# A decoder layer on one core: the last key tile turned as the fourth, a wait of GpSimd for VectorE's low half, masks on VectorE, and a written-out first trip

## The chip, the cores and the metric

One core of a Trainium2 chip. The metric is the device time of one execution in microseconds, as the median of several. The kernel is written with one hand-made instruction order for each engine: TensorE (PE), VectorE (DVE), ScalarE (ACT), GpSimd (POOL) and SyncE (SP), which issues all DMAs. Engines meet by semaphores alone.

## What is computed

A decoder layer of three blocks, each with residual and layer norm, on x of 4 x 256 x 512: a gated MLP that keeps half of the gate's entries by size, cross-attention to 4 x 1601 context rows, and a top-1 expert. The change touches the cross-attention and what stands on either side:

```
q = rmsnorm(x @ Wq.T) per head (32 heads of 128), k = rmsnorm(ctx @ Wk.T), v = ctx @ Wv.T (8 heads)
scores = q @ k.T / sqrt(128) + mask          # 256 x 1601 for each of 4 x 32 heads
out = softmax(scores) @ v, then @ Wo.T
x = layernorm(x + out)
```

## The kernel before

The program runs stage by stage: `gate_and_up`, `keys_and_values` (with the top-k counts on VectorE), `down_and_norm`, `queries`, `attention`, `output_and_experts`. A stage's loads and first steps are called inside the stage ahead of it, by functions named `early_...`.

`attention` (line 1943) works on 32 items (batch and key head), each of two units; a unit is 2 of the 4 query heads of the item, 512 query columns in four tiles j = 0 to 3 of 128. In fp16 pairs of high and low part a product is three matmuls (`product`, lines 206 to 208). For one tile j:

- TensorE scores 128 queries against all keys into four banks (`score`); these banks exist once, so the next score waits for VectorE.
- VectorE subtracts the mask and takes the minimum (`subtract_mask`, L2473), ScalarE takes the exp with its sum (`exp`, L2405).
- The probabilities have to be turned, keys onto partitions. There are NT = 13 key tiles of 128, the last with 65 keys. The first 7 go through DMA transposes in fp16: the high half is made by GpSimd for even j (L2284) or ScalarE for odd j (L2290), the low half by VectorE for even j (`halves_lo_dve`, L2294) or GpSimd for odd j (L2299), and SyncE issues a transposing DMA for each (`turn_halves`, L2184). The other 6 are turned by TensorE (`transpose_p`, L2571) into one of 3 banks, cast by ScalarE (`split_p`, L2434) and their low parts taken by VectorE (L2507).
- For the tile of the last 65 keys GpSimd repeats the keys behind the end (`repeat_tail`, L2277) and ScalarE copies the high part of 32 rows and of one row into pT_lo (L2438), so that two matmuls do for three (L2595, L2597).

The order of the loop stands in a few tables. A unit has 13 positions. At each, every engine does what the tables name. `P_AT` says at which positions the product takes a tile turned by TensorE, `TURN_AT` at which position which of the six is turned, for this unit (3, 4, 5) or the next (0, 1, 2), and `AT` where a score stands:

```python
    P_AT = (0, 1, 2, 5, 8, 11)
    AT = {0: 1, 3: 2, 6: 3, 9: 0}
    TURN_AT = {2: 3, 5: 4, 8: 5, 10: 0, 11: 1, 12: 2}
    def tile_of(pos):
        return ND + P_AT.index(pos) if pos in P_AT else D_AT.index(pos)
```

So the last key tile, number 12, is the sixth turned one (n = 5): it is turned at position 8 and multiplied at position 11, and its copies stand on ScalarE ahead of the exp of the tile j = 3. A turn of n = 0 waits for that exp.

Beside this, GpSimd prepares the items to come. In odd units (the queries' unit, p_even in the rows) it scales the queries (`scale`, L2254) and takes k_lo, q_lo, k_lo (L2247); in even ones (the values' unit, p_odd) it scales the values (`scale_v`, L2259) and takes the two v_lo and the tail (`split_tail`). Both scales stand at position 1, behind the high half of the next unit's tile 0, whose low half VectorE takes at position 0.

`schedule` runs the positions in a loop over trips of four units (BODY), the last of 16 trips written out. Before the loop, GpSimd takes k_lo, k_lo, q_lo of item 1 and then the last of eight `rows.root` (the inverse roots of the queries' norms, four pieces), and SyncE stores them. The masks are scaled on GpSimd in `early_gpsimd`, s == -2 (L2326), inside the last trip of `queries`. In the last trip SyncE issues the output stage's first seven loads in one go at unit 1, position 6 (`first_loads`), and `EARLY` says at which units and positions the first three of the output's splits stand on ScalarE and GpSimd.

Of the kernel before, what the change touches and what calls it, by code (L numbers as in the profile page):

```python
# [24 lines left out]
P = 128  # L25
B, S, D = 4, 256, 512
KV = 1601
# [1915 lines left out]
def attention(chip, mask, qS, kS, vS, rS, iS, oS, output):  # L1943
# [25 lines left out]
    P_AT = (0, 1, 2, 5, 8, 11)  # L1969
    D_AT = [pos for pos in range(NT) if pos not in P_AT]  # L1970
# [75 lines left out]
    def schedule(eng, position):  # L2046

        with eng.Fori(0, TRIPS - 1) as i:
            for u in range(BODY):
                for pos in range(NT):  # L2050
                    position(i, u, pos)
        for u in range(BODY):
            for pos in range(NT):
                position(TRIPS - 1, u, pos)

    def last_trip(i):
        return isinstance(i, int) and i == TRIPS - 1

# [14 lines left out]
    def tile_of(pos):  # L2073

        return ND + P_AT.index(pos) if pos in P_AT else D_AT.index(pos)

# [20 lines left out]
    def scalar_step(i, u, n):  # L2097

        return (NP + 2) * (BODY * i + u) + n
# [87 lines left out]
    def sync(sp):  # L2187
# [18 lines left out]
        def position(i, u, pos):  # L2206
# [14 lines left out]
            if last_trip(i) and (u, pos) == (1, 6):  # L2221
                sp.wait_ge(kq_lo, done(len(KQ) * ITEMS - 1))
                sp.wait_ge(v_lo_done, done(V_PARTS * ITEMS - 1))

                for s in range(2):
                    sp.wait_ge(o_out[s], landed(2 * (UNITS // B) // 2 - 1))
                output.early["first_loads"](sp)
# [6 lines left out]
            if pos == NT - 1:  # L2234
                store_o(i, u)

        turn_halves(sp, 0, 0, QT - 1)
        load_next_v(sp, 1)
        rows.store(sp, G // 2 - 1, 1)
        rows.stored(sp, G - 1)  # L2240
# [61 lines left out]
    def early_gpsimd(pool, s):  # L2302
# [19 lines left out]
        if s == -2:  # L2322
            guards.wait_queries(pool)
            for r in range(S // P):
                wait_apart(pool, mask_in, 16 * (2 + S // P), pool_passed)
                pool.tensor_scalar(minus_mask[:, r, 0:KV], minus_mask[:, r, 0:KV], -7e34, guards.mask_scale, ALU.max,  # L2326
                                   ALU.mult).then_inc(mask_done, 1)
# [22 lines left out]
    def gpsimd(pool):  # L2350
        def position(i, u, pos):
            after = exists(i, u + 1)
            if pos == 0 and after:
                halves_hi_pool(pool, i, u + 1, 0)
                repeat_tail(pool, i, u + 1, 0)
            if pos == 1 and splits_kq(i, u):
                scale(pool, kq_item(i, u)[0])
                split_kq_lo(pool, *kq_item(i, u), 0)
# [17 lines left out]
            if pos == 11 and splits_v(i, u):  # L2376
                split_tail(pool, *v_item(i, u))
            if last_trip(i) and u >= BODY - 3:
                output.early["gpsimd"](pool, u - BODY, pos)

        for n in range(len(KQ)):
            split_kq_lo(pool, 1, 1, n)
        rows.root(pool, G // 2 - 1, 1, range(rows.PIECES))
# [45 lines left out]
    def scalar(act):  # L2429
        def split_p(i, u, n):  # L2430
# [4 lines left out]
            if n == NP - 1:  # L2435
# [45 lines left out]
    def early_vector(dve, s):  # L2481
# [3 lines left out]
        if s == -3:  # L2485
            for n in range(1, len(KQ)):
                raw, hi, lo = KQ[n]
                dve.wait_ge(kq_hi, done(n))
                dve.tensor_tensor(lo[0], raw, hi[0], ALU.subtract).then_inc(kq_lo, 1)
        if s == 2:  # L2490
            dve.wait_ge(mask_done, 3)
            dve.wait_ge(pads, 7)
# [9 lines left out]
    def vector(dve):  # L2502
        def split_p(i, u, n):
            m, step = NP * u + n, turn_step(i, u, n)
            dve.wait_ge(pT_hi_act, done(scalar_step(i, u, n)))
            r = slice(0, P if n < NP - 1 else 96)
# [30 lines left out]

        for n in range(3):
# [23 lines left out]
    def tensor(pe):  # L2562
        def transpose_p(i, u, n):
            m, step, kt = NP * u + n, turn_step(i, u, n), ND + n
            if n == 0:
                pe.wait_ge(e_done, done(tile(i, u, QT - 1)))
            if n == NP - 1:
# [6 lines left out]
        def weigh_values(i, u, pos):  # L2574
# [13 lines left out]
            n = kt - ND  # L2588
# [49 lines left out]
def output_and_experts(chip, oS, x1S, WoT, AT, routeT, BwT, out):  # L2638
# [11 lines left out]
    EARLY = {(-3, 8): 0, (-2, 8): 1, (-1, 5): 2}  # L2650
# [77 lines left out]
    def first_loads(sp):  # L2728
        for n in range(WR):
            load_w(sp, n)  # L2730
            load_o(sp, n)
        load_o(sp, WR)
# [348 lines left out]
```

## Time and profile before

| | us |
|---|---|
| median of 3 runs | 2500.36 (2499.65 to 2502.15) |
| the profiled execution, its own time | 2498.12 |
| its span, first to last instruction | 2496.3 |
| TensorE busy | 2394.3 (96%) |
| VectorE busy | 1934.9 (78%) |
| ScalarE busy | 1607.3 (64%) |
| GpSimd busy | 1528.4 (61%) |

Busy time is that in which an engine has an instruction under way. TensorE's matmuls overlap, and their ends are modelled, so the distance between the starts of two of them tells more than the duration of one. "Idle before" in square brackets is the time for which the engine had nothing, with the instruction that let it go on. The attention stage runs from about 940 to 2290 us.

### The profile page before, as it was taken

To read this page: it belongs to the slowest core of one execution; us is meant where nothing else is said; L and a number is where in the kernel's file an instruction comes from. 1 tells how busy PE (TensorE), PEld (TensorE's weight loads), DVE (VectorE), ACT (ScalarE), POOL (GpSimd) and SP (SyncE) were. 2 spreads that over 40 slices of the span, in tenths; PEclk is the share of its full clock that TensorE was granted. 3 is DMA by queue.
4 is the path that set the end of the run, shared out by engine and by line. 5 is a ranking of instruction groups with operands and counts; after the bars stand their busy time and mean duration, and the time that the engine had idled before them with its cause. 6 is when DMAs were issued, how large, how long until landed. Compare 5 with 4: busy or idle time off the path is not lost.

```text
span 2496.3 us, 45429 instructions
## 1 busy us (share of the span) xinstructions
PE 2394.3 (96%) x12414; PEld 1646.2 (66%) x12414; DVE 1934.9 (78%) x2704; ACT 1607.3 (64%) x3248; POOL 1528.4 (61%) x1368
## 2 busy tenths in 40 slices
PE   9999999999999997999999999999999999998998
PEld 8878888888888884555555555555555555555887
DVE  5899999995874345888888888888888888884544
ACT  3177777877633555777777777777777777775321
POOL 0177778777620248777777777777777777763000
PEclk9999999999999999999999999999999999999999
DMA  6343344334464456887878787878787877867432
GB/s 230 113 124 103 114 126 126 105 112 133 130 201 131 145 183 151 170 191 176 189 178 189 177 189 176 189 174 188 176 190 180 190 184 177 191 137 217 156 107 67
DMA packets 749043, 398.32 MB, mean 160 GB/s; under 512 B 493264, under 2 KB 696144, under 8 KB 748976
## 3 DMA queue, kind: packets, MB, share of 16 engines
q1 hardware_dynamic: 748976, 397.52, 62.7%
q8 instruction: 31, 0.51, 0.1%
q14 instruction: 36, 0.29, 0.0%
HBM read 183.85 MB, written 96.11 MB: 112 GB/s over the span
## 4 chain that ended last, share of the span: by engine, by line
PE 63%; issue 11%; ACT 9%; DVE 9%; POOL 6%; DMA 1%; SPq 1%; POOLq 0%; DVEq 0%; ACTq 0%
PE banks L206 17%; PE banks L208 16%; PE banks L207 16%; PE banks L2571 5%; PE banks L1137 5%; DVE p_odd L2473 4%; DVE p_even L2473 2%; ACT p_odd L2405 2%; ACT p_even L2405 2%; ACT pT_lo L2438 2%; ACT pT_hi L2434 2%; DVE pT_lo L2507 1%; PE banks L436 1%; POOL v_sb L830 1%; ACT k_sb L914 1%
## 5 line engine op out<-in xcount | busy, mean ns | idle before, releaser
L2434 ACT CAST pT_hi<-banks 128x512 f16<-128x512 f32 x384 | 221.7, 584 | 299.8 <-PE banks L2571 298.2
L1058 DVE TENSOR_SCALAR_CACHE_REDUCE flags<-abs_s,thr 128x1376 bf16<-128x1376 f32 x256 | 403.7, 1643 | 1.1
L206 PE MATMUL banks<-k_hi,q_hi 128*128 128x416 f16 (+1 forms) x1024 | 342.7, 335 | 28.7 <-DVE t_min L2473 25.0
L207 PE MATMUL banks<-k_lo,q_hi 128*128 128x416 f16 (+1 forms) x1024 | 341.5, 334 | 0.0
L208 PE MATMUL banks<-k_hi,q_lo 128*128 128x416 f16 (+1 forms) x1024 | 341.4, 333 | 0.0
L2507 DVE TENSOR_TENSOR pT_lo<-banks,pT_hi 128x512 f16<-128x512 f32 (+1 forms) x384 | 257.8, 680 | 79.9 <-ACT pT_hi L2434 78.7
L2473 DVE CUSTOM_DVE_ANT_0 p_odd<-banks,minus_mask,guard_scalars 128x1664 f32<-128x1664 f32 x128 | 248.7, 1943 | 52.9 <-PE banks L208 52.9
L2473 DVE CUSTOM_DVE_ANT_0 p_even<-banks,minus_mask,guard_scalars 128x1664 f32<-128x1664 f32 x128 | 248.6, 1942 | 44.8 <-PE banks L208 39.3
L2405 ACT ACTIVATE p_even<-p_even,t_min 128x1601 f32<-128x1601 f32 x128 | 209.1, 1634 | 9.8 <-DVE t_min L2477 9.0
L2405 ACT ACTIVATE p_odd<-p_odd,t_min 128x1601 f32<-128x1601 f32 x128 | 209.2, 1634 | 1.1 <-DVE t_min L2477 0.2
L2299 POOL TENSOR_TENSOR halves<-p_odd,halves 128x896 f16<-128x896 f32 x64 | 120.9, 1890 | 103.3 <-ACT halves L2290 103.3
L914 ACT ACTIVATE k_sb<-banks,rstd 128x128 f32<-128x128 f32 x392 | 106.5, 383 | 116.0 <-POOL rstd L810 116.0
L206 PEld LDWEIGHTS banks<-k_hi,q_hi 128*128 128x128 f16 x1024 | 99.8, 98 | 113.3 <-DVE t_min L2473 44.1
L206 PE MATMUL banks<-pT_dma,v_hi 128*128 128x512 f16 x448 | 170.7, 381 | 3.8 <-DMA pT_dma<-halves 3.8
L207 PE MATMUL banks<-pT_dma,v_hi 128*128 128x512 f16 x448 | 170.8, 381 | 0.0
L208 PE MATMUL banks<-pT_dma,v_lo 128*128 128x512 f16 x448 | 170.7, 381 | 0.0
L2247 POOL TENSOR_TENSOR k_lo<-raw,k_hi 128x832 f16<-128x832 f32 x63 | 162.6, 2581 | 2.5 <-DVE guard_scalars L1797 2.5
L206 PE MATMUL banks<-kw_hi,c_hi 128*128 128x512 f32 x400 | 160.4, 401 | 0.8 <-DVE p_sb L350 0.3
L207 PE MATMUL banks<-kw_lo,c_hi 128*128 128x512 f32 x400 | 156.2, 391 | 0.0
L208 PE MATMUL banks<-kw_hi,c_lo 128*128 128x512 f32 x400 | 156.1, 390 | 0.0
L2299 POOL TENSOR_TENSOR halves<-p_even,halves 128x896 f16<-128x896 f32 x64 | 120.8, 1887 | 49.2 <-ACT halves L2290 49.2
L208 PEld LDWEIGHTS banks<-k_hi,q_lo 128*128 128x128 f16 x1024 | 100.3, 98 | 73.7 <-issue 0.6
(285 smaller groups left out, 6635.2 us busy)
## 6 DMA issues: line engine op xcount, KB each, us to landing
raw<-keys SPq DMA_DIRECT2D x32, 800.5 KB, 4.6
keys<-kT_sb SPq DMA_DIRECT2D x50, 512.0 KB, 4.9
values<-v_sb SPq DMA_DIRECT2D x50, 512.0 KB, 3.3
raw<-values SPq DMA_DIRECT2D x32, 768.0 KB
queries<-qT_sb SPq DMA_DIRECT2D x64, 256.0 KB, 2.7
raw<-queries SPq DMA_DIRECT2D x32, 512.0 KB, 5.3
r_sb<-query_roots SPq DMA_DIRECT2D x32, 512.0 KB, 6.5
inv_b<-inverse_sums SPq DMA_DIRECT2D x64, 256.0 KB, 3.5
```

The lines of the kernel that those rows point to most:

```text
L206: pe.matmul(out, a_hi, b_hi, start=start, stop=False)
L207: pe.matmul(out, a_hi, b_lo, start=False, stop=False)
L208: return pe.matmul(out, a_lo, b_hi, start=False, stop=stop)
L914: last = act.activation(k_sb[:, at], k_banks(s)[:, at], ACT.Copy, scale=rstd[:, s % RING, g:g + 1])
L1058: bits.done(dve.tensor_scalar(flags[:, tt % 2], abs_s[:, tt], thr[:, tt:tt + 1].bitcast(F32), 0.0, ALU.is_lt, ALU.add, accum_out=out[:, tt ...
L1137: last = pe.matmul(out, a[:, k], b, start=start and k + n == 0, stop=k == 1 and n == 2, skip_group_check=not start)
L2247: pool.tensor_tensor(lo[slot], raw, hi[slot], ALU.subtract).then_inc(lo_done, 1)
L2299: pool.tensor_tensor(halves[1][:, DW:2 * DW], p_sb[u % 2][:, j, 0:DW], halves[1][:, 0:DW], ALU.subtract).then_inc(lo_pool, 1)
L2405: act.activation(at, at, ACT.Exp, bias=t_min[:, n:n + 1], scale=-1.0, accum_out=p_sum[:, n:n + 1]).then_inc(e_done, 1)
L2434: act.copy(pT_hi[:, m % RING], t_bank(m)).then_inc(pT_hi_act, 1)
L2473: dve.tensor_tensor_reduce(banked(p_sb[u % 2][:, j, 0:KP]), psum[:, 0:SB, 0:SW], banked(minus_mask[:, j % 2]), guards.score_scale, 3.40282 ...
L2507: dve.tensor_tensor(pT_lo[r, m % RING], t_bank(m)[r], pT_hi[r, m % RING], ALU.subtract).then_inc(pT_lo_done, 1)
```

## The change

The tile of the last keys is turned as the fourth (n = 3) and with it multiplied at position 5. GpSimd waits, at position 1 of every unit in which it scales something, until VectorE has taken the first low half. The masks are scaled on VectorE. The first trip is written out, so that it can differ: in it GpSimd takes the first high half ahead of two of the three splits of item 1, VectorE takes the third (q_lo), and the last root's four pieces stand one to a unit at position 11; SyncE stores it at the end of the trip. The output's first loads go out at four places of the last trip, and `EARLY` has other places.

```diff
+    P_TILES = (7, 8, 9, 12, 10, 11)
+    TAIL_AT = P_TILES.index(NT - 1)
...
-        with eng.Fori(0, TRIPS - 1) as i:
+        for u in range(BODY):
+            for pos in range(NT):
+                position(0, u, pos)
+        with eng.Fori(1, TRIPS - 1) as i:
...
-        return ND + P_AT.index(pos) if pos in P_AT else D_AT.index(pos)
+        return P_TILES[P_AT.index(pos)] if pos in P_AT else D_AT.index(pos)
...
-        return (NP + 2) * (BODY * i + u) + n
+        return (NP + 2) * (BODY * i + u) + n + (2 if n > TAIL_AT else 0)
...
+            if last_trip(i):
+                output.early["first_loads"](sp, u, pos)
...
+            if first_trip(i) and (u, pos) == (BODY - 1, NT - 1):
+                rows.store(sp, G // 2 - 1, 1)
+                rows.stored(sp, G - 1)
...
         load_next_v(sp, 1)
-        rows.store(sp, G // 2 - 1, 1)
-        rows.stored(sp, G - 1)
...
-        if s == -2:
-            guards.wait_queries(pool)
-            for r in range(S // P):
-                wait_apart(pool, mask_in, 16 * (2 + S // P), pool_passed)
-                pool.tensor_scalar(minus_mask[:, r, 0:KV], minus_mask[:, r, 0:KV], -7e34, guards.mask_scale, ALU.max,
-                                   ALU.mult).then_inc(mask_done, 1)
...
-            if pos == 0 and after:
+            if pos == 0 and after and not (first_trip(i) and u == 0):
                 halves_hi_pool(pool, i, u + 1, 0)
                 repeat_tail(pool, i, u + 1, 0)
+            if pos == 1 and (splits_kq(i, u) or splits_v(i, u)):
+                pool.wait_ge(lo_dve, done_down(half_tile(i, u + 1, 0)))
...
+            if pos == 11 and first_trip(i):
+                rows.root(pool, G // 2 - 1, 1, range(u, u + 1))
...
-        for n in range(len(KQ)):
+        halves_hi_pool(pool, 0, 1, 0)
+        repeat_tail(pool, 0, 1, 0)
+        for n in range(2):
             split_kq_lo(pool, 1, 1, n)
-        rows.root(pool, G // 2 - 1, 1, range(rows.PIECES))
...
-            if n == NP - 1:
+            if n == TAIL_AT:
...
+        if s == -2:
+            dve.wait_ge(mask_in, 16 * (2 + S // P))
+            for r in range(S // P):
+                dve.tensor_scalar(minus_mask[:, r, 0:KV], minus_mask[:, r, 0:KV], -7e34, guards.mask_scale, ALU.max, ALU.mult
+                                  ).then_inc(mask_done, 1)
...
+        split_kq_lo(dve, 1, 1, 2)
         for n in range(3):
             split_p(0, 0, n)
...
-    EARLY = {(-3, 8): 0, (-2, 8): 1, (-1, 5): 2}
+    EARLY = {(-2, 6): 0, (-1, 3): 1, (-1, 6): 2}
...
+    FIRST_AT = {(1, 6): 0, (2, 4): 1, (2, 9): 2}
+
+    def first_loads(sp, u, pos):
+        if (u, pos) in FIRST_AT:
+            load_w(sp, FIRST_AT[u, pos])
+            load_o(sp, FIRST_AT[u, pos])
+        if (u, pos) == (3, 0):
+            load_o(sp, WR)
```

How the tail's move looks on ScalarE, in the values' unit of the loop, from position 5 on (CAST pT_hi is the cast of a turned tile, ACTIVATE the exp, CAST halves the high half of the first 7 tiles, COPY pT_lo the tail's copies). Before:

```order
L2434 CAST pT_hi<-banks 128x512 [waits pv_done]
L2405 ACTIVATE p_odd,p_sum<-p_odd,t_min 128x1601 [waits pT_hi_dve]
L2396 CAST v_hi_116<-raw 128x832 [waits pv_done,down_done]
L2398 CAST v_lo_118<-raw 128x128
L2434 CAST pT_hi<-banks 128x512 [waits pv_done]
L2438 COPY pT_lo<-pT_hi 32x512 [waits pT_hi_act]
L2438 COPY pT_lo<-pT_hi 1x512 [waits pT_hi_act]
L2405 ACTIVATE p_odd,p_sum<-p_odd,t_min 128x1601 [waits pT_hi_dve]
L2290 CAST halves_122<-p_odd 128x896 [waits pd_in1]
```

And now, in a values' unit, from position 2 on:

```order
L2443 CAST pT_hi<-banks 128x512 [waits pv_done,pT_done]
L2447 COPY pT_lo<-pT_hi 32x512 [waits pT_hi_act]
L2447 COPY pT_lo<-pT_hi 1x512 [waits pT_hi_act]
L2414 ACTIVATE p_odd,p_sum<-p_odd,t_min 128x1601 [waits pT_hi_dve]
L2300 CAST halves_122<-p_odd 128x896 [waits pd_in1,e_done]
L2405 CAST v_hi_115<-raw 128x832 [waits pv_done,down_done]
L2443 CAST pT_hi<-banks 128x512 [waits pv_done,pT_done]
L2414 ACTIVATE p_odd,p_sum<-p_odd,t_min 128x1601 [waits pT_hi_dve]
L2405 CAST v_hi_115<-raw 128x832 [waits pv_done,down_done]
L2407 CAST v_lo_117<-raw 128x128
L2443 CAST pT_hi<-banks 128x512 [waits pv_done,pT_done]
L2414 ACTIVATE p_odd,p_sum<-p_odd,t_min 128x1601 [waits pT_hi_dve]
```

The two copies stood between the cast of the sixth turned tile and the exp of tile 3; they now stand between the cast of the fourth and the exp of tile 1, ahead of the halves' cast, v_hi and the fifth tile's cast.

GpSimd in the queries' unit of the loop, from the first high half on (hT_lo_done is the count of VectorE's low halves). Before:

```order
L2284 TENSOR_SCALAR halves_121<-p_even 128x896 [waits pd_in0]
L2277 TENSOR_SCALAR p_even<-p_even 128x63 [waits e_done]
L2253 ISA
L2254 TENSOR_TENSOR raw<-raw,r_sb 128x1024 [waits q_in]
L2246 ISA
L2247 TENSOR_TENSOR k_lo_109<-raw,k_hi_107 128x2x416 [waits kq_hi]
```

And now:

```order
L2294 TENSOR_SCALAR halves_121<-p_even 128x896 [waits pd_in0]
L2287 TENSOR_SCALAR p_even<-p_even 128x63 [waits e_done]
L2361 REGISTER_ALU
L2263 ISA [waits hT_lo_done]
L2264 TENSOR_TENSOR raw<-raw,r_sb 128x1024 [waits q_in]
L2256 ISA
L2257 TENSOR_TENSOR k_lo_109<-raw,k_hi_107 128x2x416 [waits kq_hi]
```

The operations are the same; the scale and all that is queued behind it stand behind one more wait.

## Rows read from the trace of the kernel before

**Rows 1.** Windows: us; busy us (instructions) by engine; clock, DMA share, GB/s.
```profile
966.00:1010.00 44.00, 33.08 (x174) 18.01 (x173) 29.05 (x38) 28.00 (x39) 36.55 (x35) 0.92 0.69 155
...
1050.00:2200.00 1150.00, 1092.81 (x6182) 613.92 (x6181) 965.90 (x1296) 857.88 (x1181) 871.78 (x787) 1.00 0.80 183
```

**Rows 2.** Order of time, TensorE: start, duration, operation; units 1 and 60.
```profile
1000.42 0.34 PE L206 MATMUL banks<-k_hi,q_hi 128*128 128x416 f16 x1
...
2208.85 0.34 PE L206 MATMUL banks<-k_hi,q_hi 128*128 128x416 f16 x1
```

**Rows 3.** Waits in 1050 to 2200 us, TensorE: total, times, longest.
```profile
PE banks L206 <- DVE t_min L2473: 17.6, 29, 0.6
PE banks L2571 <- ACT p_odd L2405: 15.2, 28, 0.5
PE banks L206 <- DVE pT_lo L2507: 2.9, 12, 0.6
```

**Rows 4.** Order of time, TensorE, inside one item of the loop.
```profile
1502.96 0.35 PE L206 MATMUL banks<-k_hi,q_hi 128*128 128x416 f16 x1 [0.61 <-DVE t_min L2473]
...
1510.50 0.38 PE L208 MATMUL banks<-pT_dma,v_lo 128*128 128x512 f16 x1
1511.42 0.65 PE L2571 MATMUL banks<-ident,p_even 128*128 128x128 f32 x4 [0.54 <-ACT p_even L2405]
...
1513.86 0.34 PE L206 MATMUL banks<-k_hi,q_hi 128*128 128x416 f16 x1
...
1515.89 0.38 PE L206 MATMUL banks<-pT_hi,v_hi 128*128 128x512 f16 x1
...
1517.84 0.60 PE L2571 MATMUL banks<-ident,p_even 128*128 128x128 f32 x4
1518.27 0.34 PE L206 MATMUL banks<-k_hi,q_hi 128*128 128x416 f16 x1
```

**Rows 5.** Order of time, ScalarE: the tail tile's casts, then exp 3.
```profile
1507.66 0.58 ACT L2434 CAST pT_hi<-banks 128x512 f16<-128x512 f32 x1 [2.69 <-PE banks L2571]
1508.27 1.26 ACT L2438 COPY pT_lo<-pT_hi 32x512 f16<-32x512 f16 x2
1509.56 1.63 ACT L2405 ACTIVATE p_even<-p_even,t_min 128x1601 f32<-128x1601 f32 x1
```

**Rows 6.** Order of time, VectorE: first low half, in the loop and at the end.
```profile
1538.49 2.73 DVE L2294 TENSOR_TENSOR halves<-p_even,halves 128x896 f16<-128x896 f32 x1
...
2233.18 1.08 DVE L2294 TENSOR_TENSOR halves<-p_even,halves 128x896 f16<-128x896 f32 x1
```

**Rows 7.** Order of time, GpSimd: k_lo at the start; scale and k_lo in the loop.
```profile
930.87 1.79 POOL L2247 TENSOR_TENSOR k_lo<-raw,k_hi 128x832 f16<-128x832 f32 x1 [2.47 <-DVE guard_scalars L1797]
...
1537.91 2.36 POOL L2254 TENSOR_TENSOR raw<-raw,r_sb 128x1024 f32<-128x1024 f32 x1
1540.22 2.63 POOL L2247 TENSOR_TENSOR k_lo<-raw,k_hi 128x832 f16<-128x832 f32 x1
```

**Rows 8.** Start of the stage: GpSimd, TensorE; last the group of a VectorE operation.
```profile
932.77 13.19 POOL L2326 TENSOR_SCALAR minus_mask<-minus_mask,guard_scalars 128x1601 f32<-128x1601 f32 x2
...
976.90 6.46 POOL L1931 TENSOR_TENSOR row_rstd<-row_var,minus_half 128x8 f32<-128x8 f32 x4
...
948.19 0.35 PE L206 MATMUL banks<-k_hi,q_hi 128*128 128x416 f16 x1 [3.55 <-DVE t_min L2473]
...
986.08 0.61 PE L206 MATMUL banks<-pT_hi,v_hi 128*128 128x512 f16 x1 [5.98 <-DVE pT_lo L2507]
...
L2840 DVE TENSOR_SCALAR out_sb<-y_sb,mv,rstd_f 128x512 f32<-128x512 f32 x8 | 4.3, 542 | 1.5 <-POOL rstd_f L2774 1.5
```

**Rows 9.** Order of time, TensorE, last trip.
```profile
2253.95 0.58 PE L206 MATMUL banks<-pT_hi,v_hi 128*128 128x512 f16 x1 [3.58 <-DVE o_sb L2522]
...
2281.14 0.58 PE L206 MATMUL banks<-pT_dma,v_hi 128*128 128x512 f16 x1 [3.54 <-DMA pT_dma<-halves]
```

**Rows 10.** Waits of SyncE's queue, 1050 to 2200 us.
```profile
SPq L104 <- DVE halves L2294: 52.3, 56, 1.3
```

More of the change, by code:

```diff
@@ L2057, in last_trip, with first_trip @@
         return isinstance(i, int) and i == TRIPS - 1
+    def first_trip(i):
+        return isinstance(i, int) and i == 0
     def last_unit(i, u):
@@ L2226, in position @@
                     sp.wait_ge(o_out[s], landed(2 * (UNITS // B) // 2 - 1))
-                output.early["first_loads"](sp)
+            if last_trip(i):
+                output.early["first_loads"](sp, u, pos)
             if pos == 8 and after:
@@ L2505, in split_p @@
             dve.wait_ge(pT_hi_act, done(scalar_step(i, u, n)))
-            r = slice(0, P if n < NP - 1 else 96)
+            r = slice(0, 96 if n == TAIL_AT else P)
             dve.tensor_tensor(pT_lo[r, m % RING], t_bank(m)[r], pT_hi[r, m % RING], ALU.subtract).then_inc(pT_lo_done, 1)
@@ L2563, in transpose_p @@
         def transpose_p(i, u, n):
-            m, step, kt = NP * u + n, turn_step(i, u, n), ND + n
+            m, step, kt = NP * u + n, turn_step(i, u, n), P_TILES[n]
             if n == 0:
                 pe.wait_ge(e_done, done(tile(i, u, QT - 1)))
-            if n == NP - 1:
+            if n == TAIL_AT:
                 pe.wait_ge(tail_done, done(tile(i, u, QT - 1)))
@@ L2587, in weigh_values @@
                 return
-            n = kt - ND
+            n = P_AT.index(pos)
             m = NP * u + n
@@ L2726, in load_x1 @@
         sp.dma_start(x1_sb[:, t % 2], x1S[t * P:(t + 1) * P, :]).then_inc(x1_in[t % 2], 16)
[L2728 to L2732, printed above, removed]
+    FIRST_AT = {(1, 6): 0, (2, 4): 1, (2, 9): 2}
[5 more added lines that the diff above has]
+            load_o(sp, WR)
     def load_ahead(sp, n):
```

## The prediction

> **What bounds the kernel now.** I read the busy shares by stage first, then the waits inside the attention loop, then one item of it in order of time, and last the two ends of the stage. The loop is the long piece: between 1050 and 2200 us TensorE is busy 1092.8 of 1150 us, VectorE 965.9, ScalarE 857.9, GpSimd 871.8, and the DMA engines 0.80 of the time [rows 1]. So TensorE is the bound, but not all the way: a unit's first score starts at 1000.42 and, 59 units later, at 2208.85 [rows 2], so an item (two units) takes 40.96 us, and TensorE's own work is less than that. From one unit [rows 4]: a score is 2.03 us (1513.86 to 1515.89), three products 1.95, four transposes 0.43. A unit has four scores, twelve products of 0.65, the tail's short product of 0.43 and six turns: 8.12 + 7.80 + 0.43 + 2.58 = 18.93, an item 37.9. The missing 3.1 us are waits, and two kinds carry them [rows 3]: the turn of a unit's first tile waits for the last exp (28 times for p_odd, as often for p_even), and a score waits for the mask subtraction that empties its banks. The first costs more than its idle 0.54: from the product at 1510.50 to the turn at 1511.42 are 0.92 us where the next step normally starts after 0.22, so 0.70 a unit, 1.4 an item. The second is 0.61 in the unit whose GpSimd scales the queries [rows 4], some 0.8 beside the ordinary step, and 0.3 in the other; the pT_lo waits [rows 3] are another 0.3 to 0.5.
>
> **Part 1, the tail tile is turned fourth.** Before, ScalarE casts the sixth turned tile at 1507.66, makes two copies (1.26) and only then runs the exp at 1509.56 [rows 5]. That exp could start 1.29 earlier, at 1508.27, since nothing else held it. It would be over before TensorE's turn is due (0.70 later than needed now, 1.29 gained), so the 1.4 us an item go. The copies are not gone: they move behind the cast of the fourth tile, position 2, in front of exp 1, the cast for halves 1 and the q_hi or v_hi casts, and the cast of the fifth tile. There I count ScalarE from one cast to the next: 4.15 us plus the 1.4 of the copies is 5.55 in the queries' unit and 5.4 in the values' unit, where TensorE turns the next tile 4.2 later. The fifth tile's low half on VectorE then ends 0.1 (values) to 0.3 (queries) behind the moment at which the next mask subtraction could begin. Cost 0.35 an item. The tail's product (two matmuls, 0.22 shorter) moves from position 11 to 5, where the turnaround of the banks (subtraction 2.0 and some 0.36 of starting) now outlasts TensorE's 2.17 of work by 0.2 a unit: 0.4 an item, of which the plain sum above knows nothing. The tail columns are repeated 3 us before the fourth turn reads them: nothing.
>
> **Part 2, GpSimd waits for VectorE's first low half.** That low half takes 2.73 us where it starts 0.58 behind GpSimd's scale of the queries (1537.91, 2.36 long) and 1.08 in the last trip, where GpSimd has nothing to do [rows 6, 7]. Between these ends I take 1.1, since the wait makes GpSimd idle exactly then; the other end is that nothing is gained. So VectorE is 1.6 us earlier in the one unit (in the other, where it starts 0.6 behind the values' scale, about 0.9). The wait for the subtraction (0.8, 0.3) and the wait for pT_lo go, down to the 0.2 a unit named above. What it adds: GpSimd's scale starts 1.7 us later in each unit, and behind it stand k_lo, halves 1, halves 2, q_lo, k_lo and halves 3. From rows of today that chain is 15.2 us, begins 5.8 into the unit and ends 1.6 into the next, where exp 0 lets it go on at 2.9: 1.2 us of slack, so it costs nothing. In the values' unit the v_hi cast is let go 1.7 later, which ScalarE, late itself by the copies, just meets.
> The k_lo behind the scale takes 2.63 today, beside that low half, and 1.79 at 930.87 [rows 7]; the sum above uses 2.6. The Trainium skill (SBUF — State Buffer, Who interferes with whom) says that a VectorE instruction with two SBUF inputs and a GpSimd one that reads SBUF exclude each other for the whole instruction, the later one standing still. By it the low half would end one own length behind the scale: 1537.91 + 2.36 + 1.0 = 1541.3, and the trace has 1541.22. By it also k_lo falls back to 1.8 and GpSimd's slack is 2.0 and not 1.2, which makes the slow rival below rarer; the forecast needs neither.
>
> **The item after.** 37.9 + 0.4 + 0.35 = 38.65, against 40.96: 2.31 less. Over the 29.5 items between those two starts: **68 us**. The first two units of the last trip have fewer waits today: 0.5.
>
> **Part 3, masks on VectorE.** GpSimd takes 13.19 for the two [rows 8], until 945.96, and TensorE stands 3.55 before its second score at 948.19. No VectorE operation of this form and size is in the trace. Its nearest, 512 columns with two scalars, takes 0.542, so 1601 columns 1.7, two 3.4 (bounds: 2.0 at the rate of the whole-number form, 6.6 if it ran at GpSimd's pace). They would be done near 938.6, before the first score ends. The gain lies between 3.5 (this wait) and 7.4 (the mask's own advance); I take 4.5, since the queries' last projections bound the stage next. GpSimd also gets to the roots 6.5 earlier.
>
> **Part 4, roots out of the way.** The last root (0.37 and 6.46) stands between 976.5 and 983.3 before GpSimd's first half of unit 1, and TensorE waits 5.98 for it, then its clock is half: 0.50 until 991 and 0.92 on average in this stretch [rows 1, 8]. The five microseconds at half cost 2.5. All 8.5 go, but v_hi then waits for the values, whose transfers end near 981 now, and for their scale: 3.5 us return, with or without a short half clock. Net 5. Writing the first trip out costs nothing that I can see: the last trip is written out already. The roots come back one by one at position 11, 1.6 us each, into GpSimd's idle time before position 0 (at most 0.3 on VectorE). Their store and the wait for its landing block SyncE's queue once, about 2.5 us: 1.
>
> **Part 5, the output's first loads.** Today seven go out together at 2243 and the cast of the first weights waits for them in front of the first turned tiles: TensorE stands 3.58 and runs at half until 2257.5, lost 5.2; later it stands 3.54 for the halves' transposes, whose last low half sits behind wo_lo on GpSimd, again with half clock [rows 9]. Spread over the units and with the casts where no turn waits, the first goes. Of the second most stays: the last exp, two halves operations and a transposing transfer (3.0 from issue to landing) are a chain of their own, and one pair of loads now goes ahead of each of two transposes. With the earlier exp I take 8.5 in all, between 4 and 12.
>
> **Sum.** 68 + 0.5 + 4.5 + 5 - 1 + 8.5 = 85.5. Against the profiled execution's own 2498.1 (span 2496.3): 2412.6. The median of the runs shown is 2.2 above that execution, so **2415**.
>
> **Rivals.**
> A, *the queue takes over*: SyncE's transposes. Today their second one waits for VectorE's first low half (52.3 in 56 waits [rows 10]), and the DMA engines are at 0.80; at 38.65 an item that is 0.85, and some two-microsecond stretches are full now. SyncE's issues and gaps add up to about 38.1 an item by my count, only 0.5 under TensorE. For: that count; against: the low half comes sooner and frees 1.0 of it. If landings pace it at about 39.4 an item, that is 1.56 x 29.5 = 46, and the ends bring 15: 2439.
> B, *only half of it*: the copies make exp 1 and the fifth cast as late as they made exp 3, and the waits for the subtraction stay. The item gains 1.2: 35 from the loop, ends 10: 2455.
> C, *slower*: GpSimd becomes the bound. Its chain shifts onto VectorE's second low half and is stopped by it; today one such meeting stretches k_lo by 0.8 and a low half by 1.6. It decides from where the chain grows by its slack of 1.2 and by the 2.3 that would be won: 3.5 us an item. At 4.5, three bad meetings, the item is 41.9: 28 lost, 17 won at the ends: 2511. Against: nothing new overlaps there, and one old meeting ends.
> D, *it does nothing*: scale and low half are kept apart already, or the exp is held by another wait, and the ends give back in new stalls what they win: 2500.
>
> **How the numbers follow.** Forecast 0.58, its own range 2403 to 2427 (0.4 us an item either way, ends 7 to 8). A 0.2, B 0.16, C 0.03, D 0.03. Two in ten left out: 2401 to 2447 takes the forecast and A. Faster by over 0.2% (5 us, about what a measurement of this kernel can tell from none) 0.94, within 0.03, slower 0.03.
>
> **What would show it.** Right: the item at 38.6; the first low half at 1.1 and the k_lo behind the scale at 1.8; no TensorE wait for an exp in the loop; TensorE's waits there on subtractions of 0.2; masks on VectorE at 1.7 each; the stall of 5.98 gone or about 3 with another releaser; the turn of unit 62's first tile without its 3.58. Wrong: TensorE waiting in the loop for pT_dma (A) or still 0.6 for t_min (B); GpSimd without idle time in the queries' unit (C); an item over 39.5.

## The result and the profile after

| | before | after |
|---|---|---|
| median, us | 2500.01 (2498.38 to 2502.15, 4 runs) | 2433.15 (2432.23 to 2433.65, 4 runs) |
| ratio, 95% interval | | 0.9732 (0.9715 to 0.9748) |
| profiled execution: own time, span | 2498.12, 2496.3 | 2432.23, 2430.4 |

The kernel is 67 us faster, where 85.5 were forecast; the time lies 18 us above the forecast. That is inside the stated range of 2401 to 2447, but outside the 2403 to 2427 that the prediction gave its own forecast; the range reached further only to take in rival A, at 2439. Lines of the file have shifted: the turned tiles' casts are L2443, the copies L2447, the exp L2414, VectorE's low half L2304, the mask subtraction L2482, GpSimd's scale L2264, SyncE's transposes L2192.

The page of the kernel after, busy time by engine and the chain that ended last:

```profile
PE 2383.0 (98%) x12414; PEld 1650.8 (68%) x12414; DVE 1829.1 (75%) x2707; ACT 1593.3 (66%) x3248; POOL 1463.5 (60%) x1365
...
PE 45%; SPq 33%; issue 10%; DMA 8%; DVE 1%; POOL 1%; ACT 1%; POOLq 0%; ACTq 0%; DVEq 0%
```

Before, the chain gave TensorE 63% and SyncE's queue (SPq) 1%. Now a third of it runs through the queue and 8% through transfers, though TensorE is busier than ever.

The same windows as in [rows 1] (the long one ends 70 us earlier, with the loop):

```profile
966.00:1010.00 44.00, 37.32 (x203) 20.37 (x202) 30.83 (x46) 30.99 (x43) 33.49 (x34) 0.96 0.84 182
1050.00:2130.00 1080.00, 1065.71 (x6059) 606.94 (x6058) 843.54 (x1266) 824.76 (x1157) 807.57 (x771) 1.00 0.84 191
```

The starts of units 1 and 60, as in [rows 2]:

```profile
994.80 0.34 PE L206 MATMUL banks<-k_hi,q_hi 128*128 128x416 f16 x1
...
2152.17 0.34 PE L206 MATMUL banks<-k_hi,q_hi 128*128 128x416 f16 x1
```

They are 1157.37 apart instead of 1208.43: the loop gave 51, not 68. With the starts of units 0, 1, 60 and 62 both traces can be cut into pieces:

| piece | before | after | gain | forecast |
|---|---|---|---|---|
| guard scalars (VectorE) to unit 1 | 69.78 | 62.55 | 7.2 | 4.5 + 5 |
| unit 1 to unit 60, with the roots' store | 1208.43 | 1157.37 | 51.1 | 68 - 1 |
| units 60 and 61 | 39.33 | 39.99 | -0.7 | 0.5 |
| unit 62 to the end | 248.12 | 238.24 | 9.9 | 8.5 |

The guard scalars themselves come 1.6 later in the profiled execution after; they come at 930.5 to 934.2 in the 14 traces of this case, whatever the kernel. So the spans differ by 65.9. The first piece varies too between kernels whose code is the same up to unit 1 or nearly so: 69.2 to 71.2 in four with the old start (mean 70.2), 59.8 to 62.6 in nine with the new one (mean 61.2).

TensorE's waits and its weight loads' between 1040 and 2130 us, against [rows 3] (total, times, longest):

```profile
PEld banks L206 <- issue: 19.8, 30, 1.4
PE banks L206 <- DVE o_sb L2536: 9.6, 17, 1.0
PE banks L206 <- DVE t_min L2482: 0.5, 1, 0.5
```

No wait of a matmul for an exp is left and one for a subtraction (the weight loads still wait for it, 26.9 us in 100 waits). VectorE's `o_sb`, the step that empties the output bank at a unit's end, has taken their place. The weight loads' 19.8 under "issue" are the same stall: one of 0.82 stands at 1548.38, ahead of the product shown next. Where it stands, in an item of the loop:

```profile
1526.47 0.34 PE L206 MATMUL banks<-k_hi,q_hi 128*128 128x416 f16 x1
...
1545.73 0.34 PE L206 MATMUL banks<-k_hi,q_hi 128*128 128x416 f16 x1
...
1548.39 0.39 PE L206 MATMUL banks<-pT_hi,v_hi 128*128 128x512 f16 x1 [0.46 <-DVE o_sb L2536]
```

The values' unit takes 19.26 (1526.47 to 1545.73), nothing is lost in it. The queries' unit behind it starts with the stall: these units take 19.4 at best and 19.8 on average. What VectorE, SyncE and ScalarE did ahead of it (idle in brackets; SyncE's queue is written SPq):

```profile
1547.51 0.75 DVE L2536 SCALAR_TENSOR_TENSOR o_sb<-banks,guard_scalars,inv_b 128x512 f32<-128x512 f32 x1 [0.59 <-DMA inv_b<-inverse_sums]
```
```profile
1534.93 0.38 SPq L2140 DMA_DIRECT2D raw<-keys  x1
1535.51 0.36 SPq L2147 DMA_DIRECT2D raw<-queries  x1
1536.12 0.38 SPq L2148 DMA_DIRECT2D r_sb<-query_roots  x1
1536.86 1.66 SPq L2199 DMA_DIRECT2D inverse_sums<-p_invT  x4
1538.73 3.72 SPq L2192 DMA_TRANSPOSE pT_dma<-halves  x2
1543.62 0.39 SPq L2204 DMA_DIRECT2D inv_b<-inverse_sums  x1
```
```profile
1544.17 0.94 ACT L2300 CAST halves<-p_odd 128x896 f16<-128x896 f32 x1 [1.99 <-DMA pT_dma<-halves]
```

`o_sb` needs inv_b, the inverse sums, loaded from memory. That load is issued behind the second pair of transposes (tile j = 1), and this pair takes 3.72 to issue, where one elsewhere takes 2.57. The pair's landing also lets ScalarE's high half of j = 3 go, and behind that stand the three casts of the next unit. So one late pair makes two things late, and `o_sb` stands behind both: it reads inv_b, and in VectorE's order it comes after the low parts of the first two of those casts (VectorE stood 1.18 for them, then 0.59 for inv_b).

The low halves and GpSimd's scale and k_lo, against [rows 6, 7]:

```profile
1511.65 1.09 DVE L2304 TENSOR_TENSOR halves<-p_even,halves 128x896 f16<-128x896 f32 x1
```
```profile
1512.92 2.36 POOL L2264 TENSOR_TENSOR raw<-raw,r_sb 128x1024 f32<-128x1024 f32 x1 [1.77 <-DVE halves L2304]
1515.24 1.78 POOL L2257 TENSOR_TENSOR k_lo<-raw,k_hi 128x832 f16<-128x832 f32 x1
```

Start and end, against [rows 8, 9]: the masks on VectorE, the values' scale on GpSimd and TensorE behind it, and the one wait for transposes that is left in the last trip:

```profile
936.84 1.97 DVE L2502 TENSOR_SCALAR minus_mask<-minus_mask,guard_scalars 128x1601 f32<-128x1601 f32 x2
```
```profile
981.04 2.00 POOL L2269 TENSOR_SCALAR raw<-raw,guard_scalars 128x1664 f32<-128x1664 f32 x2 [6.11 <-DMA raw<-values]
```
```profile
985.23 0.39 PE L206 MATMUL banks<-pT_hi,v_hi 128*128 128x512 f16 x1 [2.98 <-DVE pT_lo L2521]
...
2217.59 0.38 PE L206 MATMUL banks<-pT_dma,v_hi 128*128 128x512 f16 x1 [1.98 <-DMA pT_dma<-halves]
```

### The profile page after: what moved, and what is told of

It is laid out like the page before. It is cut to its first block, busy times and chain, and to the rows that moved or that the text cites. A ratio compares the mean times of both kernels' runs of the same rounds, so it can differ in the third digit from the quotient of the medians.

```text
span 2430.4 us, 45071 instructions
## 1 busy us (share of the span) xinstructions
PE 2383.0 (98%) x12414; PEld 1650.8 (68%) x12414; DVE 1829.1 (75%) x2707; ACT 1593.3 (66%) x3248; POOL 1463.5 (60%) x1365
## 4 chain that ended last, share of the span: by engine, by line
PE 45%; SPq 33%; issue 10%; DMA 8%; DVE 1%; POOL 1%; ACT 1%; POOLq 0%; ACTq 0%; DVEq 0%
SPq L2192 20%; PE banks L206 12%; PE banks L208 11%; PE banks L207 11%; PE banks L1137 8%; DMA inverse_sums<-p_invT 6%; SPq L2199 3%; SPq L2163 2%; SPq L2210 2%; PE banks L436 2%; SPq L2204 1%; SPq L103 1%; SPq L2140 1%; SPq L2157 1%; SPq L104 1%
## 5 line engine op out<-in xcount | busy, mean ns | idle before, releaser
L2443 ACT CAST pT_hi<-banks 128x512 f16<-128x512 f32 x384 | 215.4, 585 | 161.9 <-PE banks L2586 160.9
L2482 DVE CUSTOM_DVE_ANT_0 p_even<-banks,minus_mask,guard_scalars 128x1664 f32<-128x1664 f32 x128 | 249.2, 1947 | 33.3 <-PE banks L208 33.2
L2482 DVE CUSTOM_DVE_ANT_0 p_odd<-banks,minus_mask,guard_scalars 128x1664 f32<-128x1664 f32 x128 | 249.4, 1948 | 30.3 <-PE banks L208 29.4
L2414 ACT ACTIVATE p_even<-p_even,t_min 128x1601 f32<-128x1601 f32 x128 | 209.3, 1635 | 3.0 <-DVE t_min L2486 2.2
L2414 ACT ACTIVATE p_odd<-p_odd,t_min 128x1601 f32<-128x1601 f32 x128 | 209.2, 1634 | 1.0 <-DVE t_min L2486 0.2
L207 PEld LDWEIGHTS banks<-k_lo,q_hi 128*128 128x128 f16 x1024 | 100.5, 98 | 61.0 <-issue 0.6
L206 PE MATMUL banks<-pT_hi,v_hi 128*128 128x512 f16 x320 | 121.6, 380 | 18.5 <-DVE o_sb L2536 9.6
## 6 DMA issues: line engine op xcount, KB each, us to landing
raw<-keys SPq DMA_DIRECT2D x32, 800.5 KB, 4.5
```

Of the source, the lines that this page charges most:

```text
L206: pe.matmul(out, a_hi, b_hi, start=start, stop=False)
L207: pe.matmul(out, a_hi, b_lo, start=False, stop=False)
L2414: act.activation(at, at, ACT.Exp, bias=t_min[:, n:n + 1], scale=-1.0, accum_out=p_sum[:, n:n + 1]).then_inc(e_done, 1)
L2443: act.copy(pT_hi[:, m % RING], t_bank(m)).then_inc(pT_hi_act, 1)
L2482: dve.tensor_tensor_reduce(banked(p_sb[u % 2][:, j, 0:KP]), psum[:, 0:SB, 0:SW], banked(minus_mask[:, j % 2]), guards.score_scale, 3.40282 ...
```

## The experiments

Twelve kernels ran, four at a time on one chip with the kernel before, so the ratios compare better than the times. Medians of 4 runs (10 for q_first_before); the item is the mean of units 10 to 59 in the trace, where everything has settled. The intervals of store_async, masks_undone and loads_undone overlap with that of the change: what is said of these three below rests on one trace each.

| kernel | us | ratio to before (95%) | item, us |
|---|---|---|---|
| before | 2497.6 to 2500.1 | | 40.88 |
| the change | 2433.15 | 0.9732 (0.9715 to 0.9748) | 39.12 |
| tail_alone | 2480.96 | 0.9922 (0.9906 to 0.9939) | 40.27 |
| wait_alone | 2456.31 | 0.9826 (0.9810 to 0.9843) | 39.43 |
| ends_alone | 2480.75 | 0.9923 (0.9906 to 0.9939) | 40.91 |
| inverse_early | 2638.88 | 1.0552 (1.0535 to 1.0570) | 46.13 |
| inv_load_late | 2563.70 | 1.0262 (1.0244 to 1.0279) | 43.70 |
| inv_idle | 2460.91 | 0.9849 (0.9833 to 0.9866) | 40.04 |
| q_first | 2417.27 | 0.9672 (0.9656 to 0.9688) | 38.68 |
| store_async | 2428.70 | 0.9718 (0.9701 to 0.9734) | 39.10 |
| q_first_before | 2495.41 | 0.9986 (0.9976 to 0.9995) | 40.76 |
| best | 2414.31 | 0.9665 (0.9649 to 0.9681) | 38.68 |
| masks_undone | 2436.37 | 0.9752 (0.9736 to 0.9769) | 39.09 |
| loads_undone | 2438.20 | 0.9760 (0.9744 to 0.9776) | 39.07 |

**One part at a time.**

tail_alone:

```diff
--- before
+    P_TILES = (7, 8, 9, 12, 10, 11)
+    TAIL_AT = P_TILES.index(NT - 1)
...
-            if n == NP - 1:
+            if n == TAIL_AT:
```

> The kernel before with the tail tile turned fourth and nothing else of the change. By the prediction's terms TensorE's wait for the last exp goes (1.4 us an item), the copies cost 0.35 and the turnaround of the banks 0.4, while the wait for the subtraction in the queries' unit stays, since the first low half still takes 2.7: an item of about 40.3 and a loop 20 us shorter, 2480. If the two parts only work together (a late low half makes the subtraction, and by it the last exp, late again), the item gains under 0.3 and the time is over 2492. If the copies cost nothing the item is 39.6, 2460.

Measured 2480.96, an item 0.61 shorter (0.65 by the terms). TensorE's waits in it, 1050 to 2150 us:

```profile
PE banks L206 <- DVE t_min L2475: 31.6, 54, 0.8
PE banks L206 <- DVE o_sb L2524: 9.5, 21, 1.7
```

The exp's waits are gone, the subtraction's have doubled against [rows 3], and the wait for `o_sb` is already there. The exp's wait had covered it: in the kernel before, 1050 to 2200 us, VectorE's `o_sb` waits for inv_b 23 times (24 in the change), but TensorE for `o_sb` only once.

```profile
DVE o_sb L2522 <- DMA inv_b<-inverse_sums: 11.0, 23, 0.6
...
PE banks L206 <- DVE o_sb L2522: 0.8, 1, 0.8
```

wait_alone:

```diff
--- before
+            if pos == 1 and (splits_kq(i, u) or splits_v(i, u)):
+                pool.wait_ge(lo_dve, done_down(half_tile(i, u + 1, 0)))
```

> The kernel before with GpSimd's wait for the first low half and nothing else of the change. By the prediction's terms the low half falls from 2.7 to 1.1, k_lo behind the scale from 2.6 to 1.8, and TensorE's waits for the subtraction and for pT_lo go: 1.2 to 1.6 us an item, with the wait for the last exp (0.54 twice an item) unchanged: 35 to 47 us, 2453 to 2465. If the exp only stands there because the subtraction is late, its wait shrinks too and the gain passes 50. If SyncE's queue holds the loop at 39.2 an item, it gets to 39.2 and no further: 2449.

Measured 2456.31, 1.45 an item. Its waits:

```profile
PE banks L2573 <- ACT p_odd L2407: 15.2, 28, 0.5
PE banks L2573 <- ACT p_even L2407: 14.7, 27, 0.6
PE banks L206 <- DVE o_sb L2524: 1.1, 1, 1.1
```

The exp's are as before, and nothing stands for the subtraction. The limit of 39.2 that the expectation named for SyncE's queue was not met here: the item stopped at 39.43 for the exp's sake.

ends_alone:

```diff
--- after
-    P_TILES = (7, 8, 9, 12, 10, 11)
+    P_TILES = (7, 8, 9, 10, 11, 12)
...
-            if pos == 1 and (splits_kq(i, u) or splits_v(i, u)):
-                pool.wait_ge(lo_dve, done_down(half_tile(i, u + 1, 0)))
```

> The changed kernel with both loop parts undone (the tail tile sixth again, GpSimd without its wait); masks on VectorE, first trip, last root and the output's first loads as in the change. The prediction put the ends at 4.5 + 5 - 1 + 8.5 = 17; the trace of the changed kernel reads 5.6 at the start of unit 1 and 9.9 behind the start of unit 62, 15.5 in all: 2484. The item should stay at 40.96. If the ends only gained because the loop's queue of waits was short, 2490 or more.

Measured 2480.75: 19.3 (the interval allows 15.3 to 23.5), item unchanged. The three parts by themselves give 19.1 + 43.8 + 19.3 = 82, close to the 85.5 forecast; together they give 67. So there is a loss of combination. Its size is less sure. By the items of the traces the two loop parts give 0.61 + 1.45 = 2.06 alone and 1.76 together, 0.30 an item or 9 us; the rest of the 15 the traces don't place, and executions of one kernel differ by up to 7 us.

**Where the combination loses: three attempts on the inverse sums.** The obvious cure was to have them earlier.

```diff
--- after
+            if pos == 2:
+                store_inverse(i, u)
             if pos == 2 and after:
                 turn_halves(sp, i, u + 1, 0)
...
             if pos == 4:
-                store_inverse(i, u)
+                load_inverse(i, u)
...
-            if pos == 6:
-                load_inverse(i, u)
...
-            if pos == 3:
+            if pos == 1:
                 invert(i, u)
```

> The changed kernel with the path of the inverse sums moved ahead: VectorE inverts at position 1 and not 3, SyncE stores the sums at position 2 ahead of the first transposes (not at 4), and loads them at 4 (not at 6, behind the second transposes). Theory Q: the 16 us that the loop lacks against the forecast are VectorE's o_sb waiting for inv_b, whose load stands in SyncE's queue behind transposes that wait; then the waits for o_sb go, the queries' units fall from 19.9 to 19.4 on average, and the time is 2433 - 16 = 2417. Theory R: ScalarE and VectorE are late by the copies, and inv_b would only be the last of several; then another wait stands in its place at once, and the time is 2429 to 2433. Theory S: the transfers' bandwidth (DMA busy 0.84) paces the loop; then the stores and loads land no earlier, and the time stays 2433.

Measured 2638.88, 206 slower than the change; none of the three theories had room for that. inv_load_late leaves the load at 6 and keeps the rest:

> As inverse_early (VectorE inverts at position 1, SyncE stores the sums at 2 ahead of the first transposes), but with the load of inv_b back at position 6, behind the second transposes. It tells which half of that edit cost 206 us. If it was the load (256 KB issued ahead of the second transposes, whose landing the trace of that run shows at 6.8 to 7.0 us instead of 3.0), the time comes back to 2420 to 2440. If it was the store (SyncE waits there for p_invT, 2.0 us on average in 47 waits, ahead of the first transposes), the time stays above 2550.

Measured 2563.70: 75 of the 206 belong to the load's place and 131 to the store's. Both halves of the edit hurt; neither sentence of the expectation held alone. The trace shows how a late queue grows so dear. The keys' loads go out 12.0 behind the unit's start instead of 8.3 (means), TensorE's stall for `o_sb` grows with them, and behind the long stall its clock is halved:

```profile
1522.56 0.39 PE L206 MATMUL banks<-pT_hi,v_hi 128*128 128x512 f16 x1 [3.59 <-DVE o_sb L2536]
...
1523.31 0.63 PE L206 MATMUL banks<-pT_hi,v_hi 128*128 128x512 f16 x1
```

From 1523.31 the matmuls start 0.43 apart instead of 0.22, for 2.6 us, at a granted clock of 0.50 (1.2 GHz), some 1.3 us lost. Over 1050 to 2250 us the clock is 0.97 on average; in inverse_early it is 0.94 (1050 to 2300), in the change and in inv_idle 1.00.

inv_idle puts the store where the queue idles:

```diff
--- after
+            if pos == 0:
+                store_inverse(i, u)
...
-            if pos == 4:
-                store_inverse(i, u)
...
-            if pos == 3:
-                invert(i, u)
+            if pos == 9 and after:
+                invert(i, u + 1)
...
+        invert(0, 0)
```

> The changed kernel, but VectorE inverts the sums of the next unit at position 9, where it idles 1.1 us, and SyncE stores them at position 0, between the store of the output and the first transposes, where its queue idles some 1.5 us; the load of inv_b stays behind the second transposes. Bytes and the number of issues are the same. Theory Q (SyncE's queue order delays inv_b): the load's wait for the stores' landing (1.1 us, 27 times) goes and the queue is up to 1.7 us earlier at the second transposes; o_sb no longer waits, 2433 - 11 to 16 = 2417 to 2422. Theory B (bytes: the second transposes are late because 1.8 MB of keys, queries and roots were issued right ahead of them): only the 1.1 us at the load go, still more than the 0.6 that o_sb waits on average, so 2420 to 2425. Theory R (VectorE or ScalarE late by the copies): 2430 to 2433.

Measured 2460.91, 28 slower. No wait for inv_b is left in the loop, and yet TensorE waits for `o_sb` four times as long as in the change (38 us in 27 waits, 1050 to 2150 us). Its queue in a values' unit that starts at 1500.71, then ScalarE, then TensorE in the queries' unit behind it:

```profile
1510.03 0.40 SPq L2140 DMA_DIRECT2D raw<-keys  x1
...
1511.85 5.66 SPq L2192 DMA_TRANSPOSE pT_dma<-halves  x2
```
```profile
1519.70 0.94 ACT L2300 CAST halves<-p_odd 128x896 f16<-128x896 f32 x1 [3.28 <-DMA pT_dma<-halves]
```
```profile
1523.24 0.39 PE L206 MATMUL banks<-pT_hi,v_hi 128*128 128x512 f16 x1 [1.08 <-DVE o_sb L2536]
```

The second transposes are issued earlier behind the loads and gain nothing by it: they take 5.66 to issue and land as late as before. By this path alone, over ScalarE's casts, the pair makes `o_sb` late. In all four traces, one values' unit each near 1500 us:

| | keys issued, from the unit's start | ScalarE let go by the second pair | behind the keys' issue |
|---|---|---|---|
| the change | 8.46 (1534.93) | 17.70 (1544.17) | 9.24 |
| inv_idle | 9.32 (1510.03) | 18.99 (1519.70) | 9.67 |
| inv_load_late | 11.62 (1509.13) | 21.52 (1519.03) | 9.90 |
| inverse_early | 11.62 (1536.91) | 22.64 (1547.93) | 11.02 |

The pair lands 9.2 to 9.9 us behind the issue of the keys, however soon it is issued itself. Keys, queries and roots are 1824.5 KB of 1024 bytes (800.5 + 512 + 512); over 9.24 us that is 202 GB/s, near the rate of the whole loop (191). With inv_b's 256 KB ahead of the pair too, it is 11.0. The other units agree: from the keys' issue to the landing of both transposes it is 9.4 on average over the 28 values' units between 1050 and 2150 us in the change, 9.8 in inv_idle and in inv_load_late, 11.3 in inverse_early. And it is 9.4 in the kernel before: the pair was as late there. So the bytes issued ahead set the landing, and what delays the loads by a microsecond (the sums' store ahead of the first transposes) delays the landing by as much. The Trainium skill (DMA: Bandwidth & Descriptors, Queues, rings and completion order) says that each DMA engine consumes its descriptors in ring order; these four rows agree.

q_first acts on the bytes and leaves the inverse sums alone:

```diff
--- after
+            if pos == 0 and not u % 2 and not last_trip(i):
+                sp.wait_ge(kq_lo, done(len(KQ) * (2 * i + u // 2 + 2) - 1))
+                load_q(sp, 2 * i + u // 2 + 2)
...
-                    load_next_kq(sp, 2 * i + u // 2 + 2)
+                    load_k(sp, 2 * i + u // 2 + 2)
```

> The changed kernel, but SyncE loads the queries and their roots (1 MB) at position 0 of the values' unit, ahead of the first transposes, and only the keys (0.8 MB) at 3. Same bytes, same number of issues. Theory B: the second transposes have 0.8 MB and not 1.8 ahead of them, their long issue (2.4 us in the trace of the changed kernel) falls to 1.2 and the load of inv_b behind them is 1.1 earlier: 2418 to 2423. The first transposes land later, by up to 4 us, and GpSimd's next high half has some 2 of slack there. Theory Q without B (only the sum of the issues counts): 2431 to 2435. If the first transposes' landing then holds the high half, slower: over 2445.

Measured 2417.27, 16 under the change and what the forecast had left. SyncE's queue, then units 28 and 29 on TensorE (19.26 and, up to 1560.27, 19.42), then TensorE's and VectorE's waits from 1040 to 2130 us:

```profile
1525.91 0.38 SPq L2147 DMA_DIRECT2D raw<-queries  x1
1526.67 0.39 SPq L2148 DMA_DIRECT2D r_sb<-query_roots  x1
1527.62 3.98 SPq L2192 DMA_TRANSPOSE pT_dma<-halves  x2
1531.87 0.36 SPq L2140 DMA_DIRECT2D raw<-keys  x1
1532.57 1.66 SPq L2199 DMA_DIRECT2D inverse_sums<-p_invT  x4
1534.43 2.57 SPq L2192 DMA_TRANSPOSE pT_dma<-halves  x2
```
```profile
1521.59 0.34 PE L206 MATMUL banks<-k_hi,q_hi 128*128 128x416 f16 x1
...
1540.85 0.34 PE L206 MATMUL banks<-k_hi,q_hi 128*128 128x416 f16 x1
```
```profile
PE banks L206 <- DVE o_sb L2539: 2.5, 4, 1.0
...
DVE o_sb L2539 <- DMA inv_b<-inverse_sums: 0.6, 1, 0.6
PE banks L206 <- DVE t_min L2485: 0.2, 1, 0.2
```

The long issue has moved to the first pair (3.98), and no wait of TensorE comes of its later landing; the second is back at 2.57 and lands 6.8 behind the keys' issue on average. The number of issues is the same, so SyncE's issue time by itself (theory Q) was not the limit.

**The control**, the same edit on the kernel before:

> The kernel before, and SyncE loads the queries and their roots at position 0 of the values' unit as in q_first. It is the control for q_first. If the second transposes behind 1.8 MB only matter once the two waits are gone (TensorE there waits for exp and subtraction, and o_sb not at all for inv_b), nothing changes: 2495 to 2503. If the order is worth 15 us by itself, whatever the rest does: 2484.

Measured 2495.41 (10 runs), 0.9986 (0.9976 to 0.9995): 3 us, 0.12 an item. The order of the loads is worth 3 us where TensorE waits for exp and subtraction, and 16 where it doesn't. The expectation says that `o_sb` doesn't wait for inv_b in the kernel before; it does (11.0 us in 23 waits, above), and TensorE has other waits at that time. The parts now add up: 0.61 + 1.45 + 0.12 = 2.18 an item, and q_first has 40.88 - 38.68 = 2.20.

**The first trip.** In the change, units 3 to 9 take 5.0 us more than at 19.42 and 19.26 a unit. store_async:

```diff
--- after
+            if not isinstance(i, int) and (u, pos) == (0, 3):
+                rows.stored(sp, G - 1)
...
             if first_trip(i) and (u, pos) == (BODY - 1, NT - 1):
                 rows.store(sp, G // 2 - 1, 1)
-                rows.stored(sp, G - 1)
```

> The changed kernel, but SyncE doesn't wait for the landing of the last roots' store at the end of the first trip; the wait stands at position 3 of the first unit of each trip of the loop, where it has long landed. In the changed kernel units 3 to 9 take 5.0 us more than the later ones. If that wait of SyncE is their cause, 4 us go: 2429. If the queue is late there from the start of the stage (the values' first loads, the fresh queue), nothing changes: 2433.

Measured 2428.70, but the trace doesn't show the expected cause: units 1 to 9 take 178.42 against 179.26, 0.8 less, and the profiled execution is 2.1 shorter ahead of unit 1, where nothing was edited. By how much that piece varies was said above. That the wait cost 4 us is not shown.

best, both edits together:

> The changed kernel with both edits that helped: queries and roots loaded at position 0 of the values' unit (q_first, 16 us under the change) and the wait for the last roots' landing put off (store_async, 4 us under it). If both add: 2412 to 2414. If q_first already took away what the late queue did in units 3 to 9: 2417.

Measured 2414.31, ratio 0.9665 (0.9649 to 0.9681): 19 under the change and the fastest kernel of the case. Units 10 to 59 are those of q_first to the hundredth; of the 3 us between the two, 1.2 lie in units 1 to 9 and the intervals overlap.

**The ends.** masks_undone scales the masks on GpSimd again:

> The changed kernel with the masks scaled on GpSimd again (13.19 us in the kernel before, 3.9 on VectorE). The prediction gave the masks 4.5 (3.5 to 7.4): 2437.6. Theory: the trace of the change shows the first exp's minimum 4.0 earlier against the guard scalars than before, of which the queries' last parts leave 3.3 at the end of unit 0: 2436.5. If it all drowns in the wait for the values' transfers at 981: 2433.

Measured 2436.37, 3.2 slower than the change. The expectation has a wrong number in it: the two masks take 1.97 on VectorE together, not 3.9. From the guard scalars to unit 1 it takes 66.38, which is 3.8 more than the change's own 62.55 and 5.2 more than the mean of nine; TensorE's stall of 3.55 ahead of the second score is back.

loads_undone issues the output's seven loads in one go and has the early splits at their old places:

> The changed kernel with the output's seven first loads in one go at unit 1, position 6 of the last trip and the early splits at their old places. The prediction gave this part 8.5 (4 to 12), the trace reads 9.9 behind the start of unit 62 together with the tail's move and the wait: 2441 to 2443. If most of the 9.9 came from the loop parts in the last units, under 2438.

Measured 2438.20: 5 by the medians, 7.7 by the trace (245.98 from unit 62 to the end instead of 238.24). The rest of the 9.9 came with the loop's parts.

## Why the prediction was right, and where it wasn't

**The item.** Forecast 38.65, measured 39.12 in the change and 38.68 in q_first, where the loads are out of the way. So the gains of part 1 and part 2 were right in mechanism and size: the low half at 1.09, k_lo at 1.78, no wait for the exp, none for the subtraction; tail_alone gave 0.61 an item where its terms make 0.65, wait_alone 1.45. What the sum had at nothing is the landing of the second transposes behind 1.8 MB of loads. The step that failed is the sum for the loop, "37.9 + 0.4 + 0.35 = 38.65", as a time that the rest of the chip would follow: 0.47 an item, 14 us of the 18. With that the forecast missed its own range; that 2433 lies in the stated one is owed to rival A's place in it, not to the forecast's mechanism.

**Rival A** had the right place and almost the right price (39.4, 39.1 measured) and 0.2 of the chance. But its mechanism was half wrong. It counted SyncE's issues, and these were not the limit; it named a wait of TensorE for pT_dma as its sign, and no such wait came. The lateness went by two side doors, inv_b's load in the same queue and ScalarE's cast for the buffer that the pair frees, and both end at `o_sb`. The clues stood in the trace of before: the DMA engines at 0.80 [rows 1], and the 23 waits for inv_b. The page of before lists landings of 3.0 for the median transpose, and a median hides one pair in eight that is late (4.7 to 5.3 there). **B** fell: no exp and no subtraction holds a product. What the copies cost no run isolates; a queries' unit takes 0.16 more than a values' one in q_first (19.42 and 19.26). **C** and **D** fell with the waits.

**GpSimd's wait.** GpSimd idles 1.77 for it in the unit shown, and no wait of TensorE in the loop names GpSimd, so the slack that part 2 counted was there.

**Start.** 9.5 forecast; 7.2 between the two profiled executions, 9.0 between the means of four and nine. The masks' 4.5 lie between the 3.8 and 5.2 of masks_undone. Their price on VectorE was put at 3.4 and is 1.97, at the prediction's lower bound of 2.0. The last root no longer holds GpSimd's first half, the values' transfers end at 981 as foretold, and TensorE stands 2.98 behind them instead of 5.98, at a granted clock of 0.96 on average in this stretch instead of 0.92 [rows 1, 8].

**The roots' store** was put at 1 us; units 3 to 9 lose 5.0 against later ones, and 3.3 of it remain in q_first, where the wait still stands. Units 3 and 4 were slow before the change as well, at 22.25 and 21.04. Whether the store or a queue that is late from the start does it stays open: store_async took 0.8 away.

**End.** 8.5 forecast, 9.9 measured, 7.7 of it by the loads and the early splits. The turn of unit 62's first tile lost its 3.58 and the wait for the halves' transposes fell from 3.54 to 1.98. Units 60 and 61 lost 0.7 instead of winning 0.5; in q_first they take 38.42, 0.9 less than before. So this too goes with the order of the loads. In the change VectorE's `o_sb` stands 1.52 for inv_b at 2154.87, whose load lands 5.4 behind its issue instead of the usual 3.5; the values and not the keys had gone out ahead of it, and why it is late there stays open.

## What to carry to other kernels

Before a wait is removed, ask which other lateness it covers: here the wait for the exp hid a load that was just as late, and two edits worth 0.61 and 1.45 us an item alone gave 1.76 together. A small transfer that someone waits for is priced by the bytes issued ahead of it, not by its own size or by the queue's issue time: look for long issues of it in the queue, and move the big loads, not the small transfer. And when an obvious cure makes things worse, as here by 206 us, its trace is the best experiment of the study.

## What the runs showed of the hardware

- A transposing DMA issued behind large loads blocks SyncE while it is issued: 1.23 us normally, up to 2.8 in the change, and 5.66 for a pair in inv_idle. A wait for a queue can so look like work of SyncE.
- The masks' operation on VectorE (fp32, 1601 columns, one constant and one scalar per partition) took 1.02 us, 0.64 ns a column; the row I had priced it by, 512 columns in 0.542 with two scalars per partition, is 1.06 ns a column. The whole-number row that gave the lower bound (L344, 1376 columns in 0.88 by the median) has the same 0.64. The Trainium skill (VectorE: DVE Perf Modes, The perf-mode tier table) gives a one-source operation from SBUF to SBUF in fp32 twice the rate of one with two sources; its 1227 ns for 2048 columns make an estimate of 0.96 for 1601 by columns alone, and the trace is near it.
- Behind a stall of 3.59 (inv_load_late, 1522.56) TensorE's granted clock was 0.50 from 1523.1 to 1525.9, and its matmuls started 0.43 apart instead of 0.22. A stall so costs more than its own length.
- The first low half of the whole stage, which has no wait in front of GpSimd's scale, took 3.00 us in the change (start 952.35, 0.34 behind the scale's start of 952.01, which ran 2.39): it ended 0.95 behind the scale's end. In the loop, where the wait stands, the 110 low halves between 1050 and 2130 us took 1.10 on average.
